# A decoder layer on one core: half of the up experts brought by SyncE's queue, up products merged into one step, second down product in four column groups, scores in tiles of 64 by 64, and a new order

## The reference, cut to what matters

```python
def layer(x, ctx):
    x = x + fourier_attention(layernorm(x))          # k, v, q = fft(x @ W.T + b); cumsum(k*v) * conj(q), normed, ifft
    x = x + cross_attention(layernorm(x), ctx, ctx)  # 16 heads of 64, causal mask and a slope per head, softmax, @ Wo
    x = x + ffn(layernorm(x))
    return x

def kmoe(x_flat, W_router, A, B, scale, bias, d_in1, d_in2, d_out1, d_out2, top_k):
    logits = x_flat @ W_router.T
    vals, idx = jax.lax.top_k(logits, top_k)              # 2 of 64 experts for each token
    probs = jax.nn.softmax(vals, axis=-1)
    xs = x_flat.reshape(-1, d_in1, d_in2)
    Ag = A[idx]
    Bg = B[idx]
    Y = jnp.einsum('nkoi,nij,nkpj->nkop', Ag, xs, Bg)
    out = jnp.einsum('nkop,nk->nop', Y, probs).reshape(-1, d_out1 * d_out2)
    return out * scale + bias

def ffn(x):                        # a token is 4 rows of 256: 64 tokens of 1024 = 32x32 per batch
    h = kmoe(x_flat, W_up, A_up, B_up, scale_up, bias_up, 32, 32, 64, 64, 2)
    h = jax.nn.gelu(h, approximate=False)
    return kmoe(h, W_down, A_down, B_down, scale_down, bias_down, 64, 64, 32, 32, 2)
```

## Time and profile before

| | |
|---|---|
| median of 3 runs | 1412.85 us |
| profiled execution, its own time | 1414.63 us |
| its span, first to last instruction | 1412.7 us |
| TensorE's mean granted clock over the span | 0.969 of full speed |
| TensorE matmul, busy | 1317.5 us |
| VectorE, busy | 1102.0 us |
| ScalarE, busy | 1081.2 us |
| GpSimd, busy | 772.4 us |

### The profile page before, as it was taken

The page is one execution under the profiler, slowest core; times in us unless marked ns, Lnnn a source line. Parts: engine busy times, 40 slices in busy tenths (PEclk is TensorE's granted clock), DMA queues, the critical chain, the costliest instruction groups (busy, mean ns, idle before and its releaser), DMA issues.

```text
span 1412.7 us, 48697 instructions
## 1 busy us (share of the span) xinstructions
PE 1317.5 (93%) x15442; PEld 1056.5 (75%) x15442; DVE 1102.0 (78%) x4099; ACT 1081.2 (77%) x3126; POOL 772.4 (55%) x2382
## 2 busy tenths in 40 slices
PE   6799999999999999999999999999999999998654
PEld 5667787877778787777878777777878777776544
DVE  1366879797987979798897979789797979888543
ACT  2457797878879697887979788897978788796732
POOL 3113647474755737375573747466473737555453
PEclk9899999999999999999999999999999999999666
DMA  9100000000000000000000000000000000000000
GB/s 287 29 16 1 17 3 17 10 10 17 10 17 3 17 10 18 9 10 17 2 17 10 17 10 11 17 10 18 2 17 10 17 10 10 10 2 10 2 9 9
DMA packets 18577, 26.04 MB, mean 18 GB/s; under 512 B 2194, under 2 KB 17171, under 8 KB 18067
## 3 DMA queue, kind: packets, MB, share of 16 engines
q1 hardware_dynamic: 18322, 22.93, 5.5%
HBM read 18.73 MB, written 4.19 MB: 16 GB/s over the span
## 4 chain that ended last, share of the span: by engine, by line
PE 53%; DVE 24%; issue 12%; ACT 4%; DVEq 2%; POOL 2%; POOLq 1%; ACTq 0%
PE P L713 8%; DVE chosen_up L336 6%; PE P L681 4%; PE X L768 4%; PE PT L768 4%; PE P L670 3%; PE G L849 3%; DVE probs L986 3%; PE F L838 3%; PE PT L733 3%; PE G L807 3%; PE X L755 3%; PE P L692 2%; PE F L867 2%; DVE chosen_dn L350 2%
## 5 line engine op out<-in xcount | busy, mean ns | idle before, releaser
L336 POOL COPY chosen_up<-experts 32x128 f32 x1024 | 358.1, 350 | 157.1 <-issue 91.9
L350 POOL COPY chosen_dn<-experts 64x64 f32 x1024 | 222.8, 273 | 198.3 <-issue 179.6
L573 ACT ACTIVATE probs<-probs,neg_max 128x128 f32<-128x128 f32 (+1 forms) x512 | 226.3, 444 | 115.4 <-DVE neg_max L986 114.3
L336 ACT COPY chosen_up<-experts 32x128 f32 x512 | 151.5, 296 | 28.7 <-PE G L849 19.7
L336 DVE COPY chosen_up<-experts 32x128 f32 x512 | 163.0, 318 | 12.7 <-issue 4.2
L986 DVE CUSTOM_DVE_ANT_0 probs<-S,distance 128x128 f32<-128x128 f32 (+1 forms) x512 | 151.7, 351 | 14.8 <-PE S L727 13.5
L733 PE MATMUL PT<-ident,probs 128*128 128x128 f32 x768 | 135.5, 285 | 7.8 <-DVE probsT L993 4.5
L612 ACT ACTIVATE hT<-h 64x1024 f32<-64x1024 f32 x64 | 126.6, 1979 | 6.7 <-DVE h L1114 5.4
L1004 DVE TENSOR_TENSOR probs<-probs,rinv 128x768 f32<-128x768 f32 x128 | 127.1, 993 | 4.4
L692 PE MATMUL P<-wv,ctxT 128*128 128x256 f32 x512 | 122.4, 382 | 0.1
L681 PE MATMUL P<-ctxT,wk 128*128 128x256 f32 x512 | 122.4, 382 | 0.0
(11 more groups left out here) (131 smaller groups left out, 2948.5 us busy)
## 6 DMA issues: line engine op xcount, KB each, us to landing
x<-in_x SPq DMA_DIRECT2D x16, 256.0 KB, 2.7
ctxT<-in_ctxT SPq DMA_DIRECT2D x16, 256.0 KB, 2.7
out<-x2b SPq DMA_DIRECT2D x16, 256.0 KB, 2.2
experts<-in_experts_up SPq DMA_DIRECT2D x2, 1024.0 KB, 19.2
wk<-in_xWk SPq DMA_DIRECT2D x1, 1024.0 KB
wo<-in_xWo SPq DMA_DIRECT2D x1, 1024.0 KB
wv<-in_xWv SPq DMA_DIRECT2D x1, 1024.0 KB, 7.6
wq<-in_xWq SPq DMA_DIRECT2D x1, 1024.0 KB, 9.7
```

The costliest lines, as they stand in the source:

```text
L336: last = copy(to[row:row + D1, n * 2 * F1:(n + 1) * 2 * F1], experts_up[k][:, bass.ds(held[g % LOADED, unit], 2 * F1)])
L350: last = copy(dst, src.rearrange("p (m c) -> p m c", m=2))
L573: act.activation(probs[:, e % 4, lo:hi], probs[:, e % 4, lo:hi], ACT.Exp, bias=neg_max[:, e % 4, rt:rt + 1], scale=-1.0, accum_out=rsum[:, ...
```

## The change

Four edits and a new table. (1) A chooser `sync` takes units 0 to 3 of each up group: SyncE's queue loads the offsets into registers and issues one DMA per unit, from the expert table in device memory straight to the slot, 16 KB each. GpSimd's share falls from four units to two, VectorE's from two to none, ScalarE keeps two. For the down layer nothing changes hands. (2) `first` and `second` are one step `up.v` for v of 0 to 8: it holds the first product of pair v and the second product of pair v-1, a token at a time in turn. The second product's output goes to the other half of the partitions, so that its weight tiles lie off the diagonal. (3) `dn_second` writes to four column groups of 32 in place of two, and `y_keep` takes them out in two copies of 64x128 in place of one of 64x256. (4) `score` makes each head's product in two halves of 64 weight columns. (5) `ORDER` is another table: it starts at another place of the cycle, and `f.2`, `k`, `v`, the Fourier part and the last `up` steps have other lags and neighbours.

```diff
-CHOOSERS = {"pool": {"up": range(0, 4), "dn": range(8, 16)},
-            "dve": {"up": range(4, 6), "dn": range(0, 4)},
+CHOOSERS = {"sync": {"up": range(0, 4), "dn": range(0)},
+            "pool": {"up": range(4, 6), "dn": range(8, 16)},
+            "dve": {"up": range(0), "dn": range(0, 4)},
             "act": {"up": range(6, 8), "dn": range(4, 8)}}
...
+choose_sync.9@3 cross.1@1 lane.1@1 up.3@3 choose_sync.10@3 choose_act.10@3 exp.6@2 choose_sync.11@3 x1_bias@2 pre.2@3
...
+            def choose(c, g):
+
+                v, half = divmod(g, 2)
+                sp.wait_ge(offsets_ready[0], c + 1)
+                fetch_offsets(at_sp, mybir.EngineType.SP, g, "sync")
+                after(sp, second_done[0], at(c, UP_PAIRS, v - UP_SLOTS + 1))
+                for unit in units:
+                    n, k = divmod(unit, TOPK)
+                    row = (1 - half) * F1 + k * D1
+                    sp.dma_start(chosen_up[v % UP_SLOTS][row:row + D1, n * 2 * F1:(n + 1) * 2 * F1],
+                                 t["experts_up"][:, bass.ds(at_sp[g % loaded(units), unit], 2 * F1)])\
+                      .then_inc(brought[v % UP_SLOTS], 16)
...
-                for s, rows in zip(S, halves):
-                    pe.matmul(s[:, 0:P], qT[rows, m, 0:P], kT[rows, m, 0:P], start=True, stop=True)
-                for s, rows in zip(S, halves):
-                    pe.matmul(s[:, P:3 * P], qT[rows, m, P:2 * P], kT[rows, m, :],
-                              start=True, stop=True).then_inc(scores_done, 1)
+                for to in halves:
+                    for s, rows in zip(S, halves):
+                        pe.matmul(s[to, 0:P], qT[rows, m, to], kT[rows, m, 0:P], start=True, stop=True)
+                for i, to in enumerate(halves):
+                    for s, rows in zip(S, halves):
+                        mm = pe.matmul(s[to, P:3 * P], qT[rows, m, P + i * KEY:P + (i + 1) * KEY], kT[rows, m, :], start=True, stop=True)
+                        if i == 1:
+                            mm.then_inc(scores_done, 1)
...
+                for p in range(UP_TOK):
+                    m, a, b, one = v * UP_TOK + p, 2 * p * F1, (2 * p + 1) * F1, slice(p * F1, (p + 1) * F1)
+                    halves = [slice(half * F1, (half + 1) * F1) for half in range(2)]
+                    if v < UP_PAIRS:
+                        for rows in halves:
+                            mm = pe.matmul(F[rows, one], own[rows, m * F1:(m + 1) * F1],
+                                           chosen_up[v % UP_SLOTS][rows, b:b + F1], start=True, stop=True)
+                        if p == UP_TOK - 1:
+                            mm.then_inc(first_done[0], 1)
+                    if w >= 0:
+                        for rows, other in zip(halves, halves[::-1]):
+                            mm = pe.matmul(G[other, one], W_up[w % 2][rows, one],
+                                           chosen_up[w % UP_SLOTS][rows, a:a + F1], start=True, stop=True)
...
-                for u in range(DN_TOK // 2):
+                for odd in (0, 1):
                     for k in range(TOPK):
-                        n = u * TOPK + k
-                        for j in (0, 1):
-                            y = G[j * D1:(j + 1) * D1, 0:DN_TOK * D1].rearrange("p (e u o) -> p u e o", e=2, o=D1)
-                            mm = pe.matmul(y[:, u], W_dn[:, (j * 8 + n) * D1:(j * 8 + n + 1) * D1],
+                        for u, j in ((odd, 0), (odd, 1), (odd + 2, 0), (odd + 2, 1)):
+                            n = u * TOPK + k
+                            to = (u // 2 * 2 + j) * D1
+                            y = G[to:to + D1, 0:4 * D1].rearrange("p (e u o) -> p u e o", e=2, o=D1)
+                            mm = pe.matmul(y[:, u % 2], W_dn[:, (j * 8 + n) * D1:(j * 8 + n + 1) * D1],
...
-                rows = DN_TOK * 4
-                dve.tensor_copy(yT[:, :, i * rows:(i + 1) * rows].rearrange("p d (n r) -> p n r d", r=4),
-                                G[0:F1, 0:DN_TOK * D1].rearrange("p (n r d) -> p n r d", r=4, d=8)).then_inc(g_kept, 1)
+                to = yT[:, :, :].rearrange("p d (i e w s) -> p i w e s d", i=DN_PAIRS, e=2, w=2)
+                for w in range(2):
+                    last = dve.tensor_copy(to[:, i, w], G[w * F1:(w + 1) * F1, 0:4 * D1].rearrange("p (e s d) -> p e s d", e=2, d=8))
+                last.then_inc(g_kept, 1)
```

More of the change, by code:

```diff
@@ L75 @@
-choose_act.18@3 catch_a.0@1 mask.1@1 turn_b.0@1 keep_up@2 dn_weigh.0@3 choose_act.19@3 exp.1@1 dn_second.0@3
-choose_dve.18@3 choose_dve.19@3 f_keep.0 score.2@1 catch_b.0@1 own_act@2 pv.0@1 choose_act.20@3 choose_pool.0@2
-choose_pool.20@3 choose_pool.21@3 choose_pool.1@2 choose_dve.0@2 choose_dve.1@2 scale.1@1 y_keep.0@3 f.1 dn_first.1@3
-turn_a.1@1 k.2@1 f_keep.1 choose_act.21@3 choose_pool.2@2 mask.2@1 catch_a.1@1 choose_act.0@2 choose_dve.20@3
-dn_weigh.1@3 dn_second.1@3 choose_dve.21@3 choose_dve.2@2 own_dve@2 choose_act.1@2 k_keep.2@1 score.3@1 y_keep.1@3
@@ L80 @@
-choose_pool.22@3 exp.2@1 dn_first.2@3 turn_b.1@1 k.3@1 v.2@1 choose_dve.22@3 choose_pool.3@2 choose_pool.4@2
-k_keep.3@1 dn_weigh.2@3 choose_act.2@2 first.0@2 keep_out.0@1 choose_act.3@2 catch_b.1@1 mask.3@1 scale.2@1 v.3@1
-turn_a.2@1 product_kv cross.0 lane.0 choose_dve.3@2 pv.1@1 exp.3@1 weigh.0@2 choose_act.22@3 choose_pool.23@3
-choose_act.23@3 dn_second.2@3 choose_dve.4@2 catch_a.2@1 choose_dve.23@3 choose_pool.5@2 scale.3@1 score.4@1
-v_keep.2@1 turn_b.2@1 choose_dve.5@2 catch_b.2@1 y_keep.2@3 mask.4@1 f.2 load_ctx turn_a.3@1 keep_out.1@1
@@ L85 @@
-choose_act.4@2 cumulate dn_first.3@3 second.0@2 dn_weigh.3@3 choose_act.5@2 choose_act.6@2 exp.4@1 pv.2@1 score.5@1
-choose_dve.6@2 pre.0@2 scale.4@1 choose_pool.6@2 catch_a.3@1 keep_out.2@1 first.1@2 choose_dve.7@2 weigh.1@2
-dn_second.3@3 turn_b.3@1 catch_b.3@1 v_keep.3@1 f_keep.2 y_keep.3@3 v.0 turn_a.4@1 second.1@2 mask.5@1 exp.5@1
-first.2@2 pv.3@1 product_q pre.1@2 catch_a.4@1 weigh.2@2 choose_pool.7@2 choose_dve.8@2 choose_act.7@2 keep_out.3@1
-scale.5@1 score.6@1 y_turn@3 final@3 turn_b.4@1 v.1 catch_b.4@1 first.3@2 second.2@2 choose_act.8@2 cross.1 mask.6@1
@@ L90 @@
-turn_a.5@1 pre.2@2 v_keep.0 exp.6@1 choose_pool.8@2 choose_pool.9@2 pv.4@1 weigh.3@2 store@3 choose_act.9@2 score.7@1
-lane.1 Q catch_a.5@1 choose_pool.10@2 choose_pool.11@2 choose_act.10@2 choose_dve.9@2 choose_dve.10@2 first.4@2
-second.3@2 scale.6@1 choose_dve.11@2 choose_pool.12@2 choose_pool.13@2 x1_bias@1 choose_pool.14@2 turn_b.5@1 k.0
-catch_b.5@1 weigh.4@2 pre.3@2 choose_pool.15@2 v_keep.1 mask.7@1 choose_act.11@2 choose_dve.12@2 choose_dve.13@2
-choose_act.12@2 keep_out.4@1 turn_a.6@1
+weigh.1@3 exp.5@2 choose_pool.6@3 choose_pool.7@3 pv.3@2 pre.0@3 turn_a.4@2 catch_a.4@2 v_keep.3@2 f.2@1 keep_out.3@2
@@ new lines @@
+catch_a.0@1 dn_first.0@3 turn_b.0@1 mask.1@1 choose_act.18@3 choose_act.19@3 spread_up@2 v.0@1 dn_weigh.0@3 keep_up@2
+choose_sync.0@2 xnT1 dn_second.0@3 exp.1@1 catch_b.0@1 choose_dve.19@3 score.2@1 dn_first.1@3 v_keep.0@1 scale.1@1
+pv.0@1 y_keep.0@3 mask.2@1 dn_weigh.1@3 choose_sync.1@2 choose_sync.2@2 choose_act.0@2 choose_sync.3@2
+choose_pool.20@3 choose_act.20@3 choose_act.21@3 choose_act.1@2 turn_a.1@1 choose_dve.20@3 f.0 dn_second.1@3
+choose_act.2@2 score.3@1 exp.2@1 choose_act.3@2 choose_dve.21@3 choose_pool.21@3 dn_first.2@3 y_keep.1@3
@@ new lines @@
+choose_dve.22@3 scale.2@1 dn_weigh.2@3 catch_a.1@1 f_keep.0 keep_out.0@1 choose_pool.22@3 choose_act.4@2
+choose_act.22@3 choose_dve.23@3 f.1 turn_b.1@1 catch_b.1@1 mask.3@1 choose_sync.4@2 choose_sync.5@2 choose_sync.6@2
+choose_sync.7@2 f_keep.1 v.1@1 turn_a.2@1 pv.1@1 choose_pool.23@3 dn_second.2@3 choose_act.23@3 choose_pool.0@2
+own_dve@2 exp.3@1 dn_first.3@3 score.4@1 y_keep.2@3 catch_a.2@1 turn_b.2@1 catch_b.2@1 dn_weigh.3@3 keep_out.1@1
+v_keep.1@1 v.2@1 scale.3@1 dn_second.3@3 pv.2@1 choose_pool.1@2 turn_a.3@1 y_keep.3@3 mask.4@1 choose_pool.2@2
@@ L95 @@
+y_turn@3 choose_pool.3@2 own_act@2 choose_pool.4@2 final@3 store@3 choose_pool.5@2 v_keep.2@1 catch_a.3@1 exp.4@1
+v.3@1 turn_b.3@1 cross.0 product_kv keep_out.2@1 lane.0 up.0@2 catch_b.3@1 weigh.0@2 score.5@1 up.1@2 choose_act.5@2
+choose_act.6@2 choose_act.7@2 scale.4@1 mask.5@1
 """
 P_USERS = ("turn1", "f", "inverse", "turn2", "k", "v", "q")
-F_USERS = ("ln3_turn", "first", "dn_first", "y_turn")
-G_USERS = ("logits_up", "spread_up", "second", "router_dn", "spread_dn", "dn_second", "y_turn")
+F_USERS = ("ln3_turn", "up", "dn_first", "y_turn")
@@ L101, in steps_in_order @@
+G_USERS = ("logits_up", "spread_up", "up", "router_dn", "spread_dn", "dn_second", "y_turn")
 def steps_in_order():
```

114 lines of the change are left out of this document (61 added, 53 removed).

## The result

| | us, median | range | against the kernel before |
|---|---|---|---|
| before | 1413.69 | 1409.89 to 1414.78, 4 runs | 1 |
| after | 1346.39 | 1343.76 to 1348.9, 4 runs | 0.952 [0.9489, 0.9552] |
| predicted | 1328 | 1292 to 1392 | 0.940 |

A forecast was written before the change was run, and what follows sets the result against it. TensorE's program, busy 98.5% of a turn, was taken as the bound. A turn of 80.9 - 7.3 + 1.1, plus 0.8 for waits, gives 75.5; 113 + 1122 + 93 = 1328 us, range 1292 to 1392.

The forecast's parts named there:

- Merged up steps: TensorE's up layer: diagonal and off-diagonal tiles run at the same time, each step costs 0.47; 3.3 us gained per turn.
- Rival B: TensorE tiles that share rows do not overlap, so merged steps cost 0.94 and scores more; 1478 us, slower, chance 0.09.
- Second down product: TensorE's `dn_second`: four column groups in place of two, 0.88 to 0.44 in 4 steps; 1.8 us gained per turn.
- Start of the scores: TensorE's scores: each 64-wide step starts faster, 8 x 0.06; 0.5 us gained per turn.
- changes of shape: TensorE's tile shape changes fall from 54 to 42 per turn, at 0.14 each; 1.7 us gained per turn.
- SyncE's wait: Before `up.7`, TensorE waits for SyncE's transfers of pairs 4 to 7; 1.1 us lost per turn.
- Rival A: SyncE's queue paces the up layer; with 0.70 us per transfer 1388 us, chance 0.17, of which 0.03 slower than before.
- Other waits: TensorE's waits on other engines rise, with ScalarE at 90% of a turn; 0.8 us added per turn, an estimate.
- VectorE's work is hidden, with 12 us to spare: In the kernel before, VectorE's work fits under TensorE's program, with 12 us of slack per turn.
- Length of the turns: The full turn falls from 80.9 to 75.5 us, 5.4 less, so fifteen turns fall from 1203 to 1122.
- Start and end: Outside the 15 turns: start stays 113 us, end falls from 97 to 93 through shorter steps at half clock.

The follow-up runs named there:

- ahead2: Changed kernel with eight up-block buffers in place of four and only pair 4's SyncE transfers moved ahead of the store and ctx load: 1336.4 us, 0.9434.
- slots8: Changed kernel with eight buffers for the up blocks in place of four, order of work unchanged: 1343.3 us, 0.9496.
- twice: Changed kernel with each of SyncE's transfers cut into two of 8 KB, 128 per turn: 1858.6 us, 1.3126.
- b_dn4: Kernel before with only the second down product put in four column groups, with the two y_keep copies it needs: 1428.7 us, 1.0088.
- b_lean_dn4: Kernel before with the second down product in four column groups and 16 of VectorE's 32 up copies per turn left out: 1375.8 us, 0.9706.
- relief: Changed kernel with merged-step alternation, four-column-group second down product and split scores all taken out: 1388.4 us, 0.98.

## Why the prediction was right, and where it was not

The forecast (1300 to 1350, 0.52) came in, by 4 us, and the sum was 18 us too low (19 by the span). Its steps:

- **Merged up steps, 3.3**: the mechanism holds, 0.47 and not 0.94 for a step of 32. A merged step measures 0.63 from start to start beside 1.08 for the pair that it replaces. Over seven that is 3.2. Rival B (1478) is out: tiles that share rows overlap here. By the rule of the Trainium skill, "TensorE: Matmul & The Clock Gate", Part 3, that the prediction weighed, the merged step would have stayed near 1.08; the rows show otherwise.
- **Second down product, 1.8**: 1.02 to 0.59, four times, 1.7.
- **Start of the scores, 0.5, and changes of shape, 1.7**: this is the term that was too large. A score fell from 0.86 to 0.70, 8 x 0.16 = 1.2, with its changes of shape in it; `dn_first` fell from 1.08 to 1.04. Together some 1.4 of 2.2. The count of changes was right, 54 to 42 by the records of a turn. The price was not: the 0.14 is the difference between a step of 0.61, with a change ahead of it and one behind it, and 0.47, so it is the price of two changes, and I charged it for each. With 0.07 the term is 0.8 and all terms together 6.4. TensorE's busy time fell by 6.6 per turn, not 7.3.
- **SyncE's wait, 1.1**: right in size, and nearly in place. The transfers are 0.57 and 0.62 apart (0.575 taken), the wait is 5.7 in six turns, at `up.6` and `up.7`, and with the waits at `up` cut to a third (`ahead2`) a turn is 1 us shorter. The reason for the late start was only in part the one given. I let the second half start as soon as `up.1` frees the slots and put the store behind all transfers; in the table the store and the load of ctx stand ahead of that half, and with eight buffers it starts only 0.7 us earlier (`slots8`). Rival A did not come, though `twice` shows its mechanism.
- **Other waits, 0.8**: right as a sum. Not busy are 2.9 us per turn, the same as in my sum (75.5 less 79.9 - 7.3).
- **VectorE's work is hidden, with 12 us to spare**: wrong as a statement on the kernel. That it hardly moved the sum is luck: the same change takes 9 us per turn off VectorE. I read VectorE's slack from its mean (69 of 81) and TensorE's bound from its busy share of 98.5%. `b_dn4`, `b_lean_dn4` and the chain show that VectorE's program set the pace in one stretch and that both engines were nearly level. Without the copies taken off VectorE, the shorter `dn_second` brings nothing in the old order, as `b_dn4` shows. The waits of the kernel before didn't give this away, as the two took turns by a few tenths of a us.
- **Length of the turns**: my turn of 75.5 against 76.2 measured, 0.7 of it work of TensorE that did not go, the term of shapes above all. But I took 5.4 off a turn of 80.9, where the median turn was 80.7, and it became 4.5; over 15 turns 66 us came off and not 81 (2 of the 15 us that are missing lie in the one turn of 78.4 with the lower clock). That is 15 of the 19 us.
- **Start and end, 113 + 93 = 206**: 108.1 + 102.2 = 210.3, against 209.7 before. The mark lies earlier in the new order, so the two must be read together: nothing was saved, where I had put 4. The end is a chain of dependent steps, with SyncE's queue in it for the last up layer, and TensorE's mean granted clock there is 0.52, against 0.66 before, so nearly all of it at the level of 1.2 GHz. What each of the two costs no run shows apart. These are the other 4 us.

One thing stays open. In the changed kernel only about half of what a TensorE step costs shows in a turn (0.6, 0.8 and 0.3 for 2.0, 1.7 and 1.2, and 2.6 for all three). The rest goes into waits that the changed kernel has anyway, 2.1 us of them per turn by `relief`. About 1 us is the wait at `up` (`ahead2`); VectorE has 16% of the chain on the page after, which hints at the other part, but no run relieved VectorE further in the changed kernel.

## What to carry to other kernels

The busy share of an engine over a turn doesn't say what slack it has: in a pipeline whose engines take their steps in a fixed order, look for the stretch in which the engine is full, and follow the chain through one turn before calling an engine hidden. Two engines can both be the bound; then an edit to one of them alone can show nothing (or a loss) and be worth its full price after the other has been relieved, so an edit that failed alone is to be tried again. Work put on a queue costs by its place in the order: look at what stands behind it, and fill the idle time ahead of a wait first.
